# Latent attention of a macaron block: scores computed twice in two layouts instead of transposed probabilities, projections as three passes over high and low parts

## The chip, the cores and the metric

One NeuronCore of one Trainium2 chip runs the whole program. The metric is device time in microseconds (us), lower is better. Five engines work in parallel, each through its own list of instructions: TensorE (PE; its weight loads are PEld), VectorE (DVE), ScalarE (ACT), GpSimd (POOL) and SyncE (SP, transfers). They wait for one another through semaphores. TensorE writes only to PSUM, eight banks of 128 partitions by 512 fp32 values; GpSimd does not read PSUM.

## The reference

The input x is [8, 512, 128] (batch, token, channel). Three stages follow one another, each with a layer norm and a residual:

```python
x = x + 0.5 * ffn(layernorm(x))      # two layers, 8 heads, local attention over windows of 64 + GLU
x = x + mla(layernorm(x))            # latent attention, causal, 16 heads of 8 channels
x = x + 0.5 * ffn(layernorm(x))
```

Only the middle stage is touched by the change. It computes, per batch element:

```python
q      = x @ W_dq.T @ W_uq.T                       # [T, 16, 8]
c_kv   = x @ W_dkv.T
q_lat  = einsum('bqhd,hdl->bhql', q, k_eff)        # k_eff = W_dq.T W_uq.T W_uk
attn   = softmax(causal(q_lat @ c_kv.T / sqrt(8))) # [16, 512, 512], key <= query
y      = einsum('bhql,hld->bqhd', attn @ c_kv, v_eff)
```

The kernel folds the weight products once, so that each head has 8 query and 8 key channels and 8 value channels.

## The kernel before

`macaron` runs a setup, `ffn_phase`, `mla_phase` and `ffn_phase` again; X stays in SBUF throughout. In the trace `mla_phase` lies from 863 to 1341.5 us of the span; the two feed-forward phases fill nearly all the rest and aren't changed.

In `mla_phase` a **group** is 4 heads of one batch element: 8 batch elements by 4 groups are 32 groups. Every engine's program is written out in the same loop over `m`, with fixed lags between the stages: `m` runs over **units**, 11 to a group. A unit is a block i of 128 queries with n heads, whose scores fill one PSUM bank: one unit for i=0 (4 heads of 128 keys), two for i=1 (2 heads of 256), four each for i=2 and i=3 (one head of 384 or 512 keys).

- Per batch element (once in four groups): layer norm on DVE (L291 to L306), 4 transposes of U (L1066), a copy to XT (L1225), values for 16 heads (L1073, copied by ACT, L1162).
- Per group: the projection of queries (L1080) and of keys (L1086), each one matmul of 512 columns with fp32 operands. To keep fp32 accuracy in the cheaper fp32r matmuls of the scores, each head's 8 channels stand several times in 128 rows, as rounded value and as what rounding leaves: ACT rounds the projection to RND (L1170, L1177), DVE subtracts (QS L1232, KL L1250). QZL is QS with all rows but one head's set to zero, four copies: two by DVE (L1242), two by POOL (L1326).
- Scores: one fp32r matmul per head over all 128 rows (L1114), and one bf16 matmul of the causal mask onto the diagonal block (L1119). The group has 4 x (128+256+384+512) = 5120 columns of scores.
- Softmax: DVE takes the negated maximum of each row (NM, L1286); ACT writes exp(score + NM) to PL (L1205), one instruction per head.
- The probabilities are turned, 128x128 by 128x128, 40 transposes per group (L1128), and copied to PTL, 9 units of 11 by ACT (L1197), two by DVE (L1295).
- Output: probabilities times values, four blocks j of 128 keys, 4 heads each in 32 columns of the array (L1143), with a column of ones that gives the sums. Then a copy OTL (L1301), 4 transposes (L1155), a reciprocal and a product (L1306, L1309) on DVE, and the addition to X on POOL (L1333).

PSUM: banks 0 to 3 are a ring of scores, 4 and 5 take transposed probabilities, bank 6 (`B_O`) the output, bank 7 (`B_PREP`) all projections and small transposes, one after another. `claim` makes PE wait, before it writes a bank, for the reader of what it held:

```python
def claim(k, name, count):
    if readers[k]:
        pe.wait_ge(*readers[k])
    readers[k] = (S[name], count)
```

## Time and profile before

| | us |
|---|---|
| median of 3 runs | 2167.96 (2165.43 to 2172.27) |
| profiled execution, its own time | 2170.55 |
| span of the profiled execution | 2168.7 |
| PE busy | 1785.8 (82%) |
| DVE busy | 1488.3 (69%) |
| ACT busy | 1112.0 (51%) |
| POOL busy | 905.7 (42%) |
| `mla_phase`, first scores to last addition | 882.4 to 1341.5 |

Busy time of PE counts a matmul from its start to its modelled end, pipelined ones overlapping; how long one occupies the array is read from the distance between the starts of two that follow one another.

### The profile page before, as it was taken

What the parts mean: (1) busy time and instruction counts of PE and PEld (TensorE: products, weight loads), DVE (VectorE), ACT (ScalarE), POOL (GpSimd) and SP (SyncE); (2) the same over time, 40 slices, a digit from 0 to 9 for tenths busy, and PEclk for the clock granted to TensorE, in tenths of its full rate; (3) what the DMA queues carried; (4) which work ended last, traced back from release to release, by engine and by line L of the source; (5) the groups of instructions that cost most, each with busy time, mean ns of one, the idle gap of its engine ahead of it and who ended that gap; (6) DMA issues with size and microseconds to landing.
All of it is one profiled execution on the core that took longest, in us unless ns stands there. A gap on an engine that the chain in (4) does not pass through costs nothing. (4 is left out here: it accounts for less than half of the span.)

```text
span 2168.7 us, 50695 instructions
## 1 busy us (share of the span) xinstructions
PE 1785.8 (82%) x20074; PEld 1079.9 (50%) x20074; DVE 1488.3 (69%) x2281; ACT 1112.0 (51%) x2070; POOL 905.7 (42%) x624
## 2 busy tenths in 40 slices
PE   1578888888888886899999997578888888888885
PEld 1344444555555543566666664344454455555543
DVE  2567777677666753688888886567777677766752
ACT  1134444454544542688888886234444454544542
POOL 2445544555445540332233321445544555445530
PEclk9889999999999998899999998689999999999998
DMA  4234434544455441000000000334344544355441
GB/s 140 37 58 71 69 62 76 77 80 69 71 79 81 73 68 36 1 1 2 1 2 1 2 1 1 37 63 72 63 71 70 81 75 74 66 85 84 84 72 40
DMA packets 66076, 119.03 MB, mean 55 GB/s; under 512 B 13183, under 2 KB 23603, under 8 KB 63667
## 3 DMA queue, kind: packets, MB, share of 16 engines
q1 hardware_dynamic: 65843, 115.79, 31.8%
q8 instruction: 162, 2.65, 0.5%
q14 instruction: 71, 0.58, 0.1%
HBM read 49.55 MB, written 3.28 MB: 24 GB/s over the span
## 5 line engine op out<-in xcount | busy, mean ns | idle before, releaser
L786 DVE SCALAR_TENSOR_TENSOR TP<-bank,cols,tab 128x1024 f32<-128x1024 f32 x256 | 318.4, 1274 | 51.5 <-PE bank L450 42.5
L946 POOL TENSOR_TENSOR QK<-QK,RB 128x1024 f32<-128x1024 f32 x128 | 302.4, 2363 | 118.6 <-DMA RB<-RN 118.6
L940 POOL TENSOR_TENSOR QK<-TP 128x512 f32<-128x512 f32 x128 | 164.9, 1289 | 327.4 <-DVE TP L786 291.3
L1205 ACT ACTIVATE PL<-bank,NM 128x384 f32<-128x384 f32 (+3 forms) x512 | 255.7, 539 | 15.8 <-DVE NM L1286 13.0
L1286 DVE TENSOR_REDUCE NM<-bank 128x1 f32<-128x384 f32 (+3 forms) x352 | 217.9, 635 | 35.6 <-PE bank L1119 31.7
L809 DVE TRANSPOSE_TENSOR_REDUCE MX<-bank 128x16 f32<-128x512 f32 x256 | 160.2, 681 | 118.3 <-PE bank L487 118.3
L642 ACT ACTIVATE SQ<-bank 128x512 f32<-128x512 f32 x128 | 76.5, 598 | 275.7 <-PE bank L450 275.5
L1128 PE MATMUL bank<-cst,PL 128*128 128x128 f32 x1280 | 199.7, 275 | 3.6 <-DVE PTL L1295 1.4
L827 DVE TENSOR_TENSOR OT<-bank,OT 128x512 f32<-128x512 f32 x128 | 85.3, 687 | 160.9 <-DMA OT<-sums_d 146.9
L1114 PE MATMUL bank<-KL,QZL 128*128 128x384 f32 (+3 forms) x512 | 189.8, 422 | 2.3 <-DVE QZL L1242 2.3
L648 ACT ACTIVATE SQ<-bank 128x512 f32<-128x512 f32 x128 | 76.5, 598 | 201.2 <-DVE TP L786 201.2
L450 PE MATMUL bank<-HTH,wqkv_h 128*128 128x512 f32 x256 | 124.3, 486 | 54.8 <-DVE TP L786 43.6
L1197 ACT ACTIVATE PTL<-bank 128x512 f32<-128x512 f32 (+1 forms) x288 | 161.5, 561 | 13.2 <-PE bank L1128 9.7
L932 POOL TENSOR_TENSOR HTL<-Z,HTH 128x512 fp32r<-128x512 f32 x32 | 37.9, 1184 | 304.4 <-ACT HTH L636 304.4
L941 POOL TENSOR_TENSOR QK<-TP 128x512 f32<-128x512 f32 x128 | 164.4, 1284 | 0.0
L1326 POOL TENSOR_SCALAR QZL<-QS,cst 128x512 fp32r<-128x512 f32 x64 | 109.2, 1715 | 116.1 <-DVE QS L1232 116.0
L520 PEld LDWEIGHTS bank<-PT,V 128*64 128x64 f32 x4096 | 128.5, 138 | 53.2 <-issue 29.4
L487 PEld LDWEIGHTS bank<-QK 32*64 32x64 f32 x8192 | 133.9, 143 | 30.0 <-issue 30.0
L520 PE MATMUL bank<-PT,V 128*64 128x64 f32 x4096 | 140.1, 224 | 10.4 <-DVE OT L827 10.2
L487 PE MATMUL bank<-QK 32*64 32x128 f32 x8192 | 146.7, 291 | 0.0
L670 ACT ACTIVATE PT<-bank 128x512 f32<-128x512 f32 x256 | 132.1, 606 | 27.7 <-PE bank L501 27.7
L1128 PEld LDWEIGHTS bank<-cst,PL 128*128 128x128 f32 x1280 | 139.1, 141 | 8.9 <-issue 5.1
(169 smaller groups left out, 3655.8 us busy)
## 6 DMA issues: line engine op xcount, KB each, us to landing
RB<-RN SPq DMA_DIRECT2D x512, 64.0 KB, 4.0
OT<-sums_d SPq DMA_DIRECT2D x128, 256.0 KB, 4.0
V<-V SPq DMA_DIRECT2D x32, 512.0 KB, 6.0
V<-V SPq DMA_DIRECT2D x32, 384.0 KB, 7.1
RB<-vars_d SPq DMA_DIRECT2D x32, 256.0 KB, 3.2
X<-in_L_attn_x SPq DMA_DIRECT2D x8, 256.0 KB, 4.6
out<-X SPq DMA_DIRECT2D x8, 256.0 KB, 4.7
wqkv_raw<-in_L_ffn_wqkv SPq DMA_DIRECT2D x1, 1536.0 KB
```

The costliest lines, as they stand in the source:

```text
L487: last = nc.tensor.matmul(BK[i][e * W:(e + 1) * W, k0:k0 + n], QK[r, 2 * g + 1, z, k0:k0 + W], QK[r, 2 * g, z, k0:k0 + n], start=False, st ...
L520: last = nc.tensor.matmul(BK[k][e * W:(e + 1) * W, w * W:(w + 1) * W], (V1, V0)[w % 2][:, w // 2, h * DH:(h + 1) * DH], PT[:, j // 2, h % ...
L786: nc.vector.scalar_tensor_tensor(out=TP[:, o:o + 2, :], in0=BK[4 + z][:, :].unsqueeze(1).to_broadcast([P, 2, T]), scalar=q, in1=tab[:, e, ...
L809: last = nc.vector.tensor_reduce(MX[:, i, :], BK[i][:, :].rearrange("p (a b) -> p a b", b=32), AX_X, ALU.max, apply_transpose=True)
L940: nc.gpsimd.tensor_tensor(QK[:, m, 0, :], TP[:, 2, :], TP[:, 1, :], ALU.subtract)
L941: nc.gpsimd.tensor_tensor(QK[:, m, 1, :], TP[:, 0, :], TP[:, 3, :], ALU.add).then_inc(S["ad_ok"], 1)
L946: nc.gpsimd.tensor_tensor(QK[:, m, :, :], QK[:, m, :, :], RB[:, m, :].unsqueeze(1).to_broadcast([P, 2, T]), ALU.mult).then_inc(S["nr_ok"], 1)
L1114: nc.tensor.matmul(bank[:, h * N:(h + 1) * N], QZL[:, G % 2, h0 + h, i * P:(i + 1) * P].bitcast(F32R), KL[:, G % 2, 0:N].bitcast(F32R), st ...
L1128: last = pe.transpose(BK[B_PT[k % 2]][:, j * P:(j + 1) * P], PL[:, k % PRING, j * P:(j + 1) * P], ident)
L1197: nc.scalar.activation(dst, src, ACT.Copy).then_inc(S["pta_ok"], 1)
L1205: last = nc.scalar.activation(PL[:, m % PRING, h * N:(h + 1) * N], BK[m % SRING][:, h * N:(h + 1) * N], ACT.Exp, bias=NM[:, m % SRING, h:h ...
L1286: nc.vector.tensor_reduce(NM[:, m % SRING, 0:n], BK[m % SRING][:, 0:n * N].rearrange("p (h k) -> p h k", h=n), AX_X, ALU.max, negate=True) ...
```

## The change

In `mla_phase`:

- **Units** are now 2 heads each over a pair of neighbouring banks (`PAIR`), 6 to a group. Fill f=0 holds query block 3 (512 keys a head), f=1 blocks 2 and 0 (384+128), f=2 block 1 (256). For the turned scores f=0 holds key block 0 (512 queries), f=1 key blocks 3 and 1 (128+384), f=2 key block 2 (256).
- **First pass** (`scores`): two bf16 masks, then the scores. Each head now has 32 rows of its own in QS and KS, so the matmul reads 32 rows of the array instead of 128; QZL is gone. DVE only takes the maxima (`maxima`, 8 instructions a group where 11 were), into NM, one column in 32.
- **Turn of the maxima**: 4 transposes (`turn_max`) and one addition to QS (`add_max`), giving QC: row 24 of each head's 32 now holds minus the maximum; KS has a 1 there (`raw_k`'s bias `one_row`).
- **Second pass** (`scores_t`), `T_LAG` = 8 units behind the first: keys by queries, KS as weights and QC moving, then two masks, last. ACT takes the exponential straight into PTL, two heads in one instruction (`softmax_exp`). PL, the 40 transposes and their copies are gone.
- **Ring**: both passes take turns in three pairs of banks (`RING` = 3). Bank 6 also takes the turned output.
- **Projections**: x and the folded weights are split into high and low fp32r parts (`high_x` on ACT, `low_x` on DVE, once a batch element; `fold_h`, `fold_l` once); queries and keys are each three fp32r matmuls of 512 columns. ACT copies the sum to RAW; POOL makes the rows (`stack_q`, `stack_k`: two instructions each), two groups ahead of their use.
- The copy to OTL is ACT's. The setup sets two small blocks of the folded weights to zero and loads a second mask.

The core of the diff (indentation cut by 16 columns; the old loop body is in the listing above):

```diff
-UNITS = [(i, h0, n) for i, n in ((i, max(1, NT // (i + 1))) for i in range(NT))
-         for h0 in range(0, LG, n)]
-UN = len(UNITS)
-ON_DVE = [0, 0, 0, 0, 0, 0, 0, 0, 1, 0, 1]
+FILLS = [((3, 0),), ((2, 0), (0, 3 * P)), ((1, 0),)]
+DIAG = [(3 * P, T), (2 * P, T), (P, 2 * P)]
+FILLS_T = [((0, 0),), ((3, 0), (1, P)), ((2, 0),)]
+DIAG_T = [(0, P), (0, 2 * P), (0, P)]
+WIDTH_T = [T, T, 2 * P]
+AT_T = {j: n * T + o for n, fill in enumerate(FILLS_T) for j, o in fill}
+READY = {j: 2 * n + 2 for n, fill in enumerate(FILLS_T) for j, o in fill}
+UN = 2 * len(FILLS)
...
-PT_LAG, PV_LAG, YT_LAG = 3, 5, 11
-EV_LAG, OT_LAG, Y_LAG = 3, 8, 11
-SRING, PRING = 4, 4
-B_PT, B_O, B_PREP = (4, 5), 6, 7
-XT_AT, Q_AT, K_AT = 1, 3, 5
-ROUND_Q, ROUND_K = 2, 4
-STEPS = ALLU + YT_LAG + 1
...
+RING = 3
+B_O, B_PREP = 6, 7
+AHEAD, QRING, KRING = 2, 3, 4
+C_AT, Q_AT, K_AT = 1, 2, 4
+XT_AT, XL_AT, V_AT, VL_AT = (AHEAD, 0), (AHEAD, 1), (AHEAD, 5), (AHEAD + 1, 0)
+T_LAG = UN + 2
+PV_LAG = {0: T_LAG + 4, 1: T_LAG + 5, 3: T_LAG + 5, 2: T_LAG + 7}
+YT_LAG, Y_LAG = T_LAG + 8, T_LAG + 9
+STEPS = ALLU + Y_LAG + 1
...
+        def project(G, s):
+            b, g = divmod(G, GROUPS)
+            terms = ((fold_h, XTH), (fold_h, XTL), (fold_l, XTH))
+            for n, (w, h) in enumerate(terms):
+                last = nc.tensor.matmul(BK[B_PREP][:, :], w[:, s, g, :].bitcast(F32R),
+                                        h[:, b % 2, :].bitcast(F32R), start=(n == 0), stop=(n == 2))
+            return last
...
-            nc.tensor.matmul(BK[B_PREP][:, :], Wq_s[:, g, :, :], XT[:, b % 2, :],
-                             start=True, stop=True).then_inc(S["q_in"], 1)
...
+            project(G, 0).then_inc(S["q_in"], 1)
...
+            lo, hi = DIAG[f]
+            for e in range(2):
+                nc.tensor.matmul(pair[:, e, lo:hi], identb[:, :],
+                                 causalb[:, :].unsqueeze(1).to_broadcast([P, (hi - lo) // P, P]),
+                                 start=True, stop=False, skip_group_check=True)
+            for i, o in FILLS[f]:
+                N = (i + 1) * P
+                for e in range(2):
+                    rows = slice(32 * (h0 + e), 32 * (h0 + e) + 32)
+                    last = nc.tensor.matmul(pair[:, e, o:o + N],
+                                            QS[rows, G % QRING, i * P:(i + 1) * P].bitcast(F32R),
+                                            KS[rows, G % KRING, 0:N].bitcast(F32R),
+                                            start=False, stop=True, skip_group_check=True)
+            last.then_inc(S["s_in"], 1)
...
+        def turn_max(G):
+            pe.wait_ge(S["nm_ok"], UN * (G + 1))
+            claim(B_PREP, "qc_ok", G + 1)
+            for i in range(NT):
+                last = pe.transpose(BK[B_PREP][:, i * P:(i + 1) * P], NM[:, G % 2, i, :], ident)
+            last.then_inc(S["c_in"], 1)
...
+        def scores_t(m):
+            G, r = divmod(m, UN)
+            f, h0 = r // 2, r % 2 * 2
+            if r == 0:
+                pe.wait_ge(S["qc_ok"], G + 1)
+            pair = PAIR[place[0] % RING]
+            claim(place[0] % RING, "ex_ok", m + 1)
+            place[0] += 1
+            lo, hi = DIAG_T[f]
+            for j, o in FILLS_T[f]:
+                N = T - j * P
+                for e in range(2):
+                    rows = slice(32 * (h0 + e), 32 * (h0 + e) + 32)
+                    nc.tensor.matmul(pair[:, e, o:o + N],
+                                     KS[rows, G % KRING, j * P:(j + 1) * P].bitcast(F32R),
+                                     QC[rows, G % 2, j * P:T].bitcast(F32R),
+                                     start=(o == 0), stop=False, skip_group_check=True)
+            for e in range(2):
+                last = nc.tensor.matmul(pair[:, e, lo:hi], identb[:, :],
+                                        causaltb[:, :].unsqueeze(1).to_broadcast([P, (hi - lo) // P, P]),
+                                        start=False, stop=True, skip_group_check=True)
+            last.then_inc(S["t_in"], 1)
...
+                scores(m)
+            if 0 <= m - T_LAG < ALLU:
+                scores_t(m - T_LAG)
+            for j in PV_LAG:
+                g = group_at(m, PV_LAG[j])
+                if g is not None:
+                    attend(g, j)
...
+            nc.scalar.activation(RAW[:, 1, :], BK[B_PREP][:, :], ACT.Identity,
+                                 bias=one_row).then_inc(S["rk_ok"], 1)
...
+        def softmax_exp(m):
+            G, r = divmod(m, UN)
+            f, h0 = r // 2, r % 2 * 2
+            act.wait_ge(S["t_in"], m + 1)
+            if r == 0 and G >= 2:
+                act.wait_ge(S["o_in"], G - 1)
+            nc.scalar.activation(PTL[:, G % 2, h0:h0 + 2, f * T:f * T + WIDTH_T[f]],
+                                 PAIR[at_t(m) % RING][:, :, 0:WIDTH_T[f]], ACT.Exp).then_inc(S["ex_ok"], 1)
...
+        def maxima(m):
+            G, r = divmod(m, UN)
+            f, h0 = r // 2, r % 2 * 2
+            dve.wait_ge(S["s_in"], m + 1)
+            if r == 0 and G < 2:
+                dve.wait_ge(S["nm_zero"], 1)
+            if r == 0 and G >= 2:
+                dve.wait_ge(S["c_in"], G - 1)
+            for i, o in FILLS[f]:
+                last = nc.vector.tensor_reduce(NM[:, G % 2, i, 24 + 32 * h0:57 + 32 * h0:32],
+                                               PAIR[at(m) % RING][:, :, o:o + (i + 1) * P],
+                                               AX_X, ALU.max, negate=True)
+            last.then_inc(S["nm_ok"], 1)
...
+        def add_max(G):
+            dve.wait_ge(S["c_in"], G + 1)
...
+            nc.vector.tensor_tensor(QC[:, G % 2, :].bitcast(F32R), BK[B_PREP][:, :], QS[:, G % QRING, :],
+                                    ALU.add).then_inc(S["qc_ok"], 1)
...
-                nc.vector.tensor_copy(dst, src).then_inc(S["ptd_ok"], 1)
...
+        def stack_q(G):
+            pool.wait_ge(S["rq_ok"], G + 1)
+            link(nc.gpsimd.tensor_scalar(HI[:, 0, :].bitcast(F32R), RAW[:, 0, :], low_q, None, ALU.mult))
+            if G >= QRING:
+                pool.wait_ge(S["qc_ok"], G - QRING + 1)
+            nc.gpsimd.tensor_tensor(QS[:, G % QRING, :].bitcast(F32R), RAW[:, 0, :], HI[:, 0, :],
+                                    ALU.subtract).then_inc(S["qs_ok"], 1)
+        def stack_k(G):
+            pool.wait_ge(S["rk_ok"], G + 1)
+            link(nc.gpsimd.tensor_scalar(HI[:, 1, :].bitcast(F32R), RAW[:, 1, :], low_k, None, ALU.mult))
+            if G >= KRING:
+                pool.wait_ge(S["t_in"], UN * (G - KRING + 1))
+            nc.gpsimd.tensor_tensor(KS[:, G % KRING, :].bitcast(F32R), RAW[:, 1, :], HI[:, 1, :],
+                                    ALU.subtract).then_inc(S["ks_ok"], 1)
...
```

TensorE in the middle of the phase, **before**: from the projection of queries to the first blocks of output. QZL and KL are the operands of scores, PL the probabilities, PTL their transposes.

```order
L1080 MATMUL bank<-XT,fold 128x512
L1114 MATMUL bank<-KL,QZL 128x384
L1119 MATMUL bank<-causalb,identb 128x128
L1128 MATMUL bank<-cst,PL 128x128 x4
L1114 MATMUL bank<-KL,QZL 128x384
L1119 MATMUL bank<-causalb,identb 128x128
L1128 MATMUL bank<-cst,PL 128x128 x4
L1143 MATMUL bank<-PTL,VL 32x512 x4
L1086 MATMUL bank<-XT,fold 128x512
```

The same engine and place **in the changed program**, two steps of the loop (r = 2, with the projection of queries, and r = 3), up to the block of output behind them:

```order
L1093 MATMUL banks<-XTH,fold_h 128x512
L1093 MATMUL banks<-XTL,fold_h 128x512
L1093 MATMUL banks<-XTH,fold_l 128x512
L1121 MATMUL banks<-causalb,identb 128x256 x2
L1128 MATMUL banks<-KS,QS 128x384 x2
L1128 MATMUL banks<-KS,QS 128x128 x2
L1154 MATMUL banks<-QC,KS 128x512 x2
L1159 MATMUL banks<-causaltb,identb 128x128 x2
L1121 MATMUL banks<-causalb,identb 128x256 x2
L1128 MATMUL banks<-KS,QS 128x384 x2
L1128 MATMUL banks<-KS,QS 128x128 x2
L1154 MATMUL banks<-QC,KS 128x512 x2
```

The transposes of PL between the units are gone; each step has a unit of the first pass and one of the second, whose score matmuls stand next to each other, with masks on either side.

VectorE in the changed program, one group with no layer norm in it (L1325 is `add_max`, L1315 `maxima`, L1331 and L1334 the result):

```order
L1325 TENSOR_TENSOR QC<-banks,QS 128x512
L1315 TENSOR_REDUCE NM<-banks 128x2 x6
L1331 RECIPROCAL RL<-banks 128x16
L1334 TENSOR_TENSOR Y<-banks,RL 128x128
L1315 TENSOR_REDUCE NM<-banks 128x2 x2
```

Before, VectorE's list for a group held 11 such reductions, two copies to PTL, QS, KL, two QZL and OTL as well.

## Rows read from the trace of the kernel before

**Rows 1.** The page, part 1: busy time, share of the span, instructions.

```profile
PE 1785.8 (82%) x20074; PEld 1079.9 (50%) x20074; DVE 1488.3 (69%) x2281; ACT 1112.0 (51%) x2070; POOL 905.7 (42%) x624
```

**Rows 2.** Stretches: length, busy PE, PEld, DVE, ACT, POOL, clock, DMA, GB/s.

```profile
872.00:900.00 28.00, 22.87 (x110) 14.84 (x111) 17.46 (x39) 16.43 (x39) 7.52 (x5) 0.73 0.00 1
1100.00:1200.00 100.00, 98.90 (x772) 62.87 (x771) 84.23 (x169) 87.40 (x191) 29.51 (x23) 1.00 0.01 2
```

**Rows 3.** Line L1080, weight loads: min/median/max ns, first and last start.

```profile
L1080 PEld LDWEIGHTS bank<-XT,fold x64: 190/192/353, 874.5 to 1310.0; 128*128 128x128 f32 x64
```

**Rows 4.** Line L1333, the addition to X: min/median/max ns, first and last start.

```profile
L1333 POOL TENSOR_TENSOR X<-X,Y x32: 451/457/463, 909.9 to 1341.0; 128x128 f32<-128x128 f32 x32
```

**Rows 5.** Timeline of PE, start of the phase: start us, us, instruction.

```profile
869.78 1.11 PE L1066 MATMUL bank<-cst,U 128*128 128x128 f32 x4 [7.49 <-DVE U L306]
...
882.42 1.08 PE L1114 MATMUL bank<-KL,QZL 128*128 128x128 f32 x4 [2.31 <-DVE QZL L1242]
```

**Rows 6.** Timeline of PE, within one group in the middle of the phase.

```profile
1100.08 1.07 PE L1143 MATMUL bank<-PTL,VL 128*32 128x512 f32 x8
...
1101.08 1.12 PE L1086 MATMUL bank<-XT,fold 128*128 128x512 f32 x2
...
1102.22 0.23 PE L1119 MATMUL bank<-causalb,identb 128*128 128x128 bf16 x1
...
1103.95 0.50 PE L1128 MATMUL bank<-cst,PL 128*128 128x128 f32 x3
...
1104.38 0.64 PE L1143 MATMUL bank<-PTL,VL 128*32 128x256 f32 x8
...
1104.95 0.50 PE L1114 MATMUL bank<-KL,QZL 128*128 128x512 f32 x1
...
1107.45 0.47 PE L1114 MATMUL bank<-KL,QZL 128*128 128x512 f32 x1
1107.77 0.23 PE L1119 MATMUL bank<-causalb,identb 128*128 128x128 bf16 x1
1107.83 0.60 PE L1128 MATMUL bank<-cst,PL 128*128 128x128 f32 x4
1108.28 0.60 PE L1155 MATMUL bank<-cst,OTL 128*128 128x128 f32 x4
1108.63 0.64 PE L1114 MATMUL bank<-KL,QZL 128*128 128x128 f32 x4
1109.11 0.39 PE L1119 MATMUL bank<-causalb,identb 128*128 128x512 bf16 x1
1109.34 0.60 PE L1128 MATMUL bank<-cst,PL 128*128 128x128 f32 x4
```

**Rows 7.** Timeline of PE, first feed-forward phase: scores in small tiles of the array.

```profile
400.94 2.03 PE L487 MATMUL bank<-QK 32*64 32x128 f32 x128
402.90 1.07 PE L509 MATMUL bank<-PT,ones 128*32 128x512 f32 x8
```

**Rows 8.** The same phase: fp32r matmuls of 512 columns, four starts apart.

```profile
428.24 0.39 PE L450 MATMUL bank<-HTL,wqkv_h 128*128 128x512 f32 x1
...
429.18 0.40 PE L450 MATMUL bank<-HTH,wqkv_l 128*128 128x512 f32 x1
```

**Rows 9.** DVE by line and form, 900 to 1300 us: count, busy us, mean ns.

```profile
L1286 DVE TENSOR_REDUCE NM<-bank 128x1 f32<-128x512 f32 x112 | 73.0, 684 | 22.2 <-PE bank L1119 22.2
L1286 DVE TENSOR_REDUCE NM<-bank 128x1 f32<-128x384 f32 x113 | 62.3, 551 | 1.9
```

**Rows 10.** Timeline of DVE: three reductions in a row.

```profile
1135.70 1.88 DVE L1286 TENSOR_REDUCE NM<-bank 128x1 f32<-128x512 f32 x3
```

**Rows 11.** ACT by line and form, 900 to 1300 us.

```profile
L1205 ACT ACTIVATE PL<-bank,NM 128x512 f32<-128x512 f32 x112 | 77.8, 695 | 2.3 <-DVE NM L1286 1.7
```

**Rows 12.** POOL by line and form: L1326 from 868 to 1325 us.

```profile
L1326 POOL TENSOR_SCALAR QZL<-QS,cst 128x512 fp32r<-128x512 f32 x64 | 109.2, 1715 | 116.1 <-DVE QS L1232 116.0
```

**Rows 13.** POOL by line and form: L932, first feed-forward phase.

```profile
L932 POOL TENSOR_TENSOR HTL<-Z,HTH 128x512 fp32r<-128x512 f32 x16 | 18.9, 1184 | 150.9 <-ACT HTH L636 150.9
```

More of the change, by code:

```diff
@@ L49, in shape_constants @@
     causal = np.where(np.arange(P)[None, :] <= np.arange(P)[:, None], 0.0, BIG).astype(np.float32)
-    headsel = row % (LG * DG) // DG == np.arange(LG)[None, :]
-    low = [-1.0 * (row // (LG * DG) >= 2), -1.0 * (row // (LG * DG) % 2)]
+    part = row % 32 // DG
+    split = [part == 2, part == 1, row % 32 == 24]
     hsum = row // 32 == np.arange(32)[None, :] // 8
@@ L1008, in mla_phase, with group_at, at, at_t @@
+                def group_at(m, lag):
+                    G, r = divmod(m - lag, UN)
+                    return G if r == 0 and 0 <= G < ALLG else None
+                def at(m):
+                    return m + max(0, m - T_LAG)
+                def at_t(m):
+                    return min(m + T_LAG + 1, ALLU) + m
                 U = sb("U", [P, 2, NT, P])
                 fold = sb("fold", [P, 2 * GROUPS * P + P])
[L1010 removed]
@@ L1089, in _, with turn_out @@
+                        def turn_out(G):
+                            claim(B_O, "y_ok", G + 1)
+                            for t in range(NT):
+                                last = pe.transpose(BK[B_O][:, t * P:(t + 1) * P], OTL[:, t * P:(t + 1) * P], ident)
+                            last.then_inc(S["y_in"], 1)
                         xt(0)
                         pe.wait_ge(S["fold_in"], 16)
+                        for G in range(AHEAD):
+                            queries(G)
+                            keys(G)
@@ new lines, in _ @@
+                            if batch_at(m, VL_AT):
+                                values(batch_at(m, VL_AT))
+                            g = group_at(m, YT_LAG)
+                            if g is not None:
+                                turn_out(g)
+                            if r == Q_AT + 1 and G + AHEAD < ALLG:
+                                raw_q(G + AHEAD)
+                            if r == K_AT + 1 and G + AHEAD < ALLG:
+                                raw_k(G + AHEAD)
+                            if 0 <= m - T_LAG < ALLU:
+                                softmax_exp(m - T_LAG)
```

402 lines of the change are left out of this document (171 added, 231 removed).

## Prediction

> **What bounds the kernel now.** The page first: no engine fills the span, PE comes nearest with 82% [rows 1]. Only `mla_phase` changes, so its stretch is read by itself: between 1100 and 1200 us PE is busy 98.90 of 100 us at full clock, DVE 84.23, ACT 87.40, POOL 29.51 [rows 2]. PE never rests, so a group costs what PE needs for it. The first query projection loads its weights at 874.5, the last group's at 1310.0, 31 groups on [rows 3]: 14.05 us a group. From the first scores at 882.42 [rows 5] to the end of the last addition, 1341.0 + 0.46 [rows 4], are 459.0 us: 32 x 14.05 = 449.6 and 9.4 of lead and tail.
>
> **Prices on PE** are distances between starts. An fp32r matmul of 512 columns: (429.18 - 428.24) / 4 = 0.235 [rows 8]. A transpose: eight from 1107.83 to 1108.63, 0.10 each. A mask of 512 columns: 1109.34 - 1109.11 = 0.23. A score matmul of 512 columns behind a transpose: 0.32, so 0.08 of weight loading shows. Four of 128 columns: 1109.11 - 1108.63 = 0.48, 0.12 each, double the 0.06 of streaming: weights bound them. The fp32 projection: 1102.22 - 1101.08 = 1.14, less 0.26 for the score matmul of 384 columns between (0.32 less a quarter of 0.235), is 0.88. Output block of 256 columns: 1104.95 - 1104.38 = 0.57, of 512: 1101.08 - 1100.08 = 1.00; so 0.43 for each 256 columns and 0.14 fixed. In front of it three transposes from 1103.95 end by 1104.25, the block starts at 1104.38: 0.13 [rows 6]. The fixed 0.13 to 0.14 on either side is what I call a change of tile shape.
>
> Test on the old group: 44 transposes 4.4; scores and masks 4 x 0.38 + 4 x 0.32 + 2 x 0.44 + 0.71 = 4.4; output 1.00 + 0.78 + 0.57 + 0.35 and four entries of 0.13, 3.2; two projections 1.76; a quarter of the batch element's transposes and values, some 0.35. Sum 14.1 against 14.05: the prices hold.
>
> **The new group on PE.**
> - Transposes: 40 go, 4 come (the maxima), 4 stay: 8 x 0.10 = 0.80.
> - Projections: 6 x 0.235 = 1.41 instead of 1.76.
> - Masks: two passes of 2048 columns: 8 x 0.235 = 1.88.
> - Scores: 10240 columns, one after another 20 x 0.235 = 4.70. But two heads of a unit use different 32 rows of the array and different banks. No row of before has tiles of 32 x 128, so this is bounded. One end: no overlap, 4.70. The other: both heads at once, 2.35. The nearest row speaks for overlap: L487 has 64 fp32 matmuls in 32 x 64 tiles, 7680 columns, which at 0.88 for 512 would take 13.2 us in a row; they took 402.90 - 400.94 = 1.96, 6.7 times less with eight tiles [rows 7]. I take 2.35, and 0.25 for the 128-column ones.
> - Shape changes: since the masks of the second pass stand last, both passes' scores are adjacent, so a step has two changes, not four: 12 x 0.13 = 1.56.
> - Output: 2.70 as before, three blocks to enter instead of four: 2.9 in all. Batch share 0.35.
>
> Sum: 0.80 + 1.41 + 1.88 + 2.35 + 0.25 + 1.56 + 2.9 + 0.35 = 11.5 us.
>
> **The other engines must fit under that.** DVE: a reduction of 512 columns is 0.684, of 384 0.551, so 1.04 ns a column [rows 9], and in a row they follow every 0.60 (1.88 for three, the last one full) [rows 10]. One of 1024 then costs 1.13, f=1 (768 and 256 columns) 1.20, f=2 0.60; twice each 5.9. `add_max` 0.7, result 0.6, norm work, XT and the low part of x about 1.2 a group: 8.4. Two copies to PTL, QS, KL, QZL and OTL are gone. ACT: four exponentials of 1024, at most twice 0.695 [rows 11], two of 512, three copies: under 9.1. POOL: twice 1.72 + 1.18 [rows 12, 13] and 0.46 [rows 4]: 6.3; it works two groups ahead, so this is hidden, and if it came late the first scores of a group would wait. None bounds the group.
>
> **Waits.** `scores_t` of step m writes the pair that `scores` of m-1 had, so it waits for that maximum. It is tight where two f=1 units follow (r=2 to 3): the maximum comes 0.15 + 1.20 + 0.1 = 1.45 after the scores; PE has `scores_t` (0.235 + 0.12 + 0.13) and the next masks and scores (0.23 + 0.13 + 0.30) = 1.15 to do first, so it stands 0.3. Where norm work (0.3 to 0.45 a step, in every second group) lies between the reductions, 0.4 more there and some at r=5 to 0. Once a batch element DVE's XT, ACT's high part and DVE's low part stand in line before `add_max`: 0.5. Mean over groups: 0.6. `scores` of m waits for the exponential of m-2, at most 1.4, with over a step between: nothing. So 12.1 us a group.
>
> **Ends.** The lead changes little: x is split (ACT 0.6, DVE 0.7) and POOL makes rows in two times 2.9 in place of DVE's 0.75, but values come later: first scores near 881 instead of 882.4. The first 8 steps have no second pass and run at DVE's 1.2 a step instead of 2.0, 6.6 less; the last 8 units of the second pass with output and addition add 13.7. 7.1 in all instead of 9.4. Setup and feed-forward phases stay.
>
> **Sum.** 32 x (14.05 - 12.1) = 62.4, ends 2.3, start 1.4: 66 us off the profiled execution's 2170.55, 2104.5. The median is 2.6 lower, so **2102 us**. Within 0.3% (6.5 us) a measurement of this kernel can't tell a change.
>
> **A rule against it.** The shape change measured 0.13 [rows 6]. The Trainium skill, TensorEngine Tiling (Array Packing), Key Properties, says that changing the tiling mode drains TensorE; a full drain is the second rival below. At 0.13 a side the rows show less than that, though for 128 x 32 tiles only.
>
> **Rivals.**
> - *Waits small*: if weight loads hide behind the neighbouring head and waits cost nothing, 11.3 a group: 88 + 3.7 less, 2076. The 6.7-fold overlap [rows 7] speaks for it, the f=1 steps against.
> - *Full drain*: every change costs a transpose's time from start to end (0.60 for four, less three starts of 0.10: 0.30 [rows 6]) instead of 0.13: 12 x 0.17 = 2.0 more, PE then waits for nothing else, 13.5 a group: 2168 - 18 - 3.7, 2146. Output blocks of before speak against it.
> - *Maxima late*: the reductions over two banks or the exponentials come later than priced, 12.8 a group: 40 + 3.7 less, 2124. DVE's list has no slack at r=2 and 3.
> - *No overlap of heads*: 4.70 + 0.5 for scores, 14.1 to 14.2 with waits hidden: 2168 within 6. The change then doesn't do what 32-row tiles are there for. Rows 7 speak against it.
> - *Lockstep in the ring, slower*: three pairs for two passes. If each step is PE's first-pass fill, wait, maximum, second-pass fill one after another (0.65 + 0.15 + 1.0 + 0.1 + 0.55 = 2.45 a step, everything else hidden), a group is 14.7: 21 more, less 3.7 at the ends, 2185. It decides from 14.05 / 6 = 2.34 us a step. Against it: `scores` of m doesn't need the maximum of m-1, so PE can fill ahead.
>
> **Chances.** Forecast (11.7 to 12.4 a group, 2090 to 2114) 0.45, waits small 0.2, maxima late 0.18, full drain 0.06, no overlap 0.04, lockstep 0.07. All but the last two are faster: 0.89; same 0.04; slower 0.07. The range takes in the forecast, most of the small-wait and of the late-maxima case: 2080 to 2135.
>
> **What would show it.** `mla_phase` from first scores to last addition 394 us; distance of two `turn_max` 12.1; PE busy near all of it at clock 1.00 (in the lead it is 0.73 [rows 2] and should be so again); score matmuls of a pair starting far closer than 0.235 apart; PE waiting for NM at the second f=1 step and hardly elsewhere; DVE near 70%, ACT near 65%, POOL 50%. I am wrong if the pair starts 0.235 apart, if a shape change costs 0.3, or if PE waits for NM or PTL in every step.

## The result and the profile after

The changed kernel takes 2141.97 us (median of 3 runs, 2140.03 to 2146.62) against 2167.96: ratio 0.988, 95% interval 0.9852 to 0.9908, 26 us faster. The forecast was 2102, range 2080 to 2135. The sign is right, the gain is 40% of what was forecast, and the time lies outside the range. The profiled execution took 2146.62 with a span of 2144.8.

The page of the changed kernel, part 1, answers to [rows 1]:

```profile
PE 1746.9 (81%) x19914; PEld 1024.5 (48%) x19914; DVE 1369.1 (64%) x2002; ACT 938.8 (44%) x1503; POOL 979.3 (46%) x692
```

Stretches of the changed kernel (length, busy PE, PEld, DVE, ACT, POOL, clock, DMA, GB/s); the first two are those of [rows 2]:

```profile
872.00:900.00 28.00, 17.09 (x53) 10.01 (x54) 9.78 (x26) 5.46 (x8) 19.95 (x15) 0.54 0.06 22
1100.00:1200.00 100.00, 93.44 (x789) 53.15 (x789) 63.33 (x116) 53.74 (x73) 50.14 (x41) 0.98 0.00 1
...
880.00:900.00 20.00, 15.34 (x45) 8.88 (x46) 5.43 (x11) 4.40 (x7) 17.32 (x14) 0.50 0.00 1
900.00:920.00 20.00, 19.88 (x88) 10.61 (x87) 12.92 (x24) 6.46 (x8) 10.59 (x8) 0.50 0.00 1
920.00:940.00 20.00, 18.41 (x126) 10.24 (x122) 9.05 (x15) 7.93 (x11) 6.08 (x5) 0.78 0.00 1
940.00:960.00 20.00, 19.53 (x174) 11.06 (x174) 13.32 (x27) 10.95 (x15) 8.91 (x7) 1.00 0.00 1
```

Two things show. In the middle PE has 6.6 us of idle time in 100, where before it had 1.1. And from 880 to 920 the granted clock is 0.50 (1.2 GHz), even in the 20 us from 900 in which PE is busy 19.88, and from 920 to 940 still 0.78. Before, with its first scores at 882.42, it was back at 1.00 by 888:

```profile
884.00:888.00 4.00, 4.00 (x17) 2.36 (x17) 3.49 (x11) 2.84 (x9) 0.62 (x1) 0.59 0.00 0
888.00:892.00 4.00, 3.53 (x23) 2.29 (x22) 4.00 (x9) 3.80 (x9) 3.79 (x3) 1.00 0.00 0
```

The turn of the maxima (L1138, `turn_max`) happens once a group, so the distance between two of them is the time of a group. Here are four of them in the middle of the phase, in the PE timeline of the changed kernel. PE stood longest ahead of the third, for XT, and ahead of L1085, the matmuls that make a batch element's values:

```profile
1055.02 0.66 PE L1138 MATMUL banks<-cst,NM 128*128 128x128 f32 x4
...
1067.13 0.66 PE L1138 MATMUL banks<-cst,NM 128*128 128x128 f32 x4
...
1080.80 0.63 PE L1138 MATMUL banks<-cst,NM 128*128 128x128 f32 x4 [0.68 <-DVE XT L1297]
...
1091.27 1.13 PE L1085 MATMUL banks<-fold,XT 128*128 128x128 f32 x8 [1.35 <-ACT RAW L1235]
...
1095.24 0.66 PE L1138 MATMUL banks<-cst,NM 128*128 128x128 f32 x4
```

The distances are 12.11, 13.67 and 14.44; the next one, which completes the four groups of a batch element, is 11.98. A **plain** group costs 11.98 or 12.12 by turns, 12.05 on average. The two groups in which the next batch element is prepared cost 13.67 and 14.43, together 4.0 more. The first two distances of the phase are 17.02 and 17.79.

Why PE waits 1.35 for ACT stands in ACT's timeline there. The key projection was finished about 1088.4. ACT copied it (L1235) only at 1090.45, behind the exponential of the projection's own step (L1244), and that exponential had waited for its scores:

```profile
1089.53 1.02 ACT L1244 ACTIVATE PTL<-banks 128x1024 f32<-128x1024 f32 x1 [1.00 <-PE banks L1159]
1090.45 0.68 ACT L1235 ACTIVATE RAW<-banks,cst 128x512 f32<-128x512 f32 x1
```

The prices within a plain group, PE timeline (answers to [rows 6]):

```profile
1097.70 0.50 PE L1093 MATMUL banks<-XTH,fold_h 128*128 128x512 f32 x1
1098.04 0.39 PE L1093 MATMUL banks<-XTL,fold_h 128*128 128x512 f32 x1
1098.27 0.40 PE L1093 MATMUL banks<-XTH,fold_l 128*128 128x512 f32 x1
1098.51 0.39 PE L1121 MATMUL banks<-causalb,identb 128*128 128x256 bf16 x2
1098.83 0.50 PE L1128 MATMUL banks<-KS,QS 32*128 32x384 f32 x4
1099.17 0.45 PE L1154 MATMUL banks<-QC,KS 32*128 32x512 f32 x2
1099.55 0.28 PE L1159 MATMUL banks<-causaltb,identb 128*128 128x128 bf16 x2
1099.67 0.38 PE L1121 MATMUL banks<-causalb,identb 128*128 128x256 bf16 x2
1099.98 0.51 PE L1128 MATMUL banks<-KS,QS 32*128 32x384 f32 x4
1100.72 0.49 PE L1154 MATMUL banks<-QC,KS 32*128 32x512 f32 x2 [0.23 <-DVE NM L1315]
```

Three passes of a projection take 0.81 (1097.70 to 1098.51). Both heads' first-pass scores, 1024 columns, take 0.34 (1098.83 to 1099.17); at 0.235 for 512 they would take 0.47 if one followed the other. Two masks with the change of shape behind them take 0.32, and PE waits for a maximum once, 0.23, in the second f=1 step.

### The profile page after: what moved, and what is told of

The parts are those of the page before. It is cut to its first block and busy times, and to the rows that moved or that the text cites. A ratio compares the mean times of both kernels' runs of the same rounds, so it can differ in the third digit from the quotient of the medians.

```text
span 2144.8 us, 48275 instructions
## 1 busy us (share of the span) xinstructions
PE 1746.9 (81%) x19914; PEld 1024.5 (48%) x19914; DVE 1369.1 (64%) x2002; ACT 938.8 (44%) x1503; POOL 979.3 (46%) x692
## 3 DMA queue, kind: packets, MB, share of 16 engines
q8 instruction: 160, 2.62, 0.5%
## 5 line engine op out<-in xcount | busy, mean ns | idle before, releaser
L793 DVE SCALAR_TENSOR_TENSOR TP<-banks,cols,tab 128x1024 f32<-128x1024 f32 x256 | 318.3, 1274 | 52.5 <-PE banks L457 46.5
L1315 DVE TENSOR_REDUCE NM<-banks 128x2 f32<-128x1024 f32 (+3 forms) x256 | 202.9, 820 | 129.4 <-PE banks L1128 129.4
L1244 ACT ACTIVATE PTL<-banks 128x1024 f32<-128x1024 f32 (+1 forms) x192 | 168.1, 884 | 192.9 <-PE banks L1159 190.5
L816 DVE TRANSPOSE_TENSOR_REDUCE MX<-banks 128x16 f32<-128x512 f32 x256 | 160.2, 682 | 122.3 <-PE banks L494 122.3
L649 ACT ACTIVATE SQ<-banks 128x512 f32<-128x512 f32 x128 | 76.6, 599 | 279.1 <-PE banks L457 278.8
L655 ACT ACTIVATE SQ<-banks 128x512 f32<-128x512 f32 x128 | 76.7, 599 | 200.3 <-DVE TP L793 200.3
L527 PEld LDWEIGHTS banks<-PT,V 128*64 128x64 f32 x4096 | 128.6, 138 | 52.9 <-issue 29.5
L494 PEld LDWEIGHTS banks<-QK 32*64 32x64 f32 x8192 | 136.3, 145 | 30.3 <-issue 30.3
L494 PE MATMUL banks<-QK 32*64 32x128 f32 x8192 | 149.2, 294 | 0.0
L527 PE MATMUL banks<-PT,V 128*64 128x64 f32 x4096 | 140.2, 224 | 9.9 <-DVE OT L834 9.7
L677 ACT ACTIVATE PT<-banks 128x512 f32<-128x512 f32 x256 | 132.4, 609 | 27.7 <-PE banks L508 27.4
```

The source lines that it names most:

```text
L494: last = nc.tensor.matmul(BK[i][e * W:(e + 1) * W, k0:k0 + n], QK[r, 2 * g + 1, z, k0:k0 + W], QK[r, 2 * g, z, k0:k0 + n], start=False, st ...
L527: last = nc.tensor.matmul(BK[k][e * W:(e + 1) * W, w * W:(w + 1) * W], (V1, V0)[w % 2][:, w // 2, h * DH:(h + 1) * DH], PT[:, j // 2, h % ...
L677: nc.scalar.activation(PT[:, g, i, :], BK[i][:, :], ACT.Exp).then_inc(S["ex_ok"], 1)
L793: nc.vector.scalar_tensor_tensor(out=TP[:, o:o + 2, :], in0=BK[4 + z][:, :].unsqueeze(1).to_broadcast([P, 2, T]), scalar=q, in1=tab[:, e, ...
L816: last = nc.vector.tensor_reduce(MX[:, i, :], BK[i][:, :].rearrange("p (a b) -> p a b", b=32), AX_X, ALU.max, apply_transpose=True)
L1244: nc.scalar.activation(PTL[:, G % 2, h0:h0 + 2, f * T:f * T + WIDTH_T[f]], PAIR[at_t(m) % RING][:, :, 0:WIDTH_T[f]], ACT.Exp).then_inc(S[" ...
```

## The experiments

Twelve more kernels ran. Ratios are to runs of the kernel before that were taken together with each, so ratios compare better than medians. **Phase** is the distance from VectorE's first statistics of `mla_phase` to the start of the last turn of maxima: it leaves out the feed-forward phases, whose code no kernel here touches. Phase and distances come from one profiled execution of each kernel; the change and e8 are the same kernel, and their phases differ by 1.1. "First two distances" are those between the first three turns of maxima.

| run | median us | ratio [95%] | phase us | first two distances, us |
|---|---|---|---|---|
| the change | 2141.97 | 0.988 [0.9852, 0.9908] | 436.0 | 17.02, 17.79 |
| e8 change again | 2139.79 | 0.9855 [0.9813, 0.9897] | 434.9 | 17.02, 16.96 |
| e1 values later | 2128.55 | 0.9802 [0.9771, 0.9832] | 424.3 | 17.01, 14.07 |
| e2 e1 and XT first | 2122.08 | 0.977 [0.974, 0.9801] | 419.9 | 17.02, 13.97 |
| e6 copies early | 2122.91 | 0.9756 [0.9724, 0.9788] | 414.3 | 16.80, 13.57 |
| e3 the change, lead filled | 2135.12 | 0.9831 [0.9799, 0.9863] | 435.8 | 17.02, 17.75 |
| e9 e6, first 8 steps filled | 2117.19 | 0.9743 [0.9714, 0.9772] | 407.9 | 10.52, 12.89 |
| e7 e6, lead and steps filled | 2109.80 | 0.9701 [0.9673, 0.9728] | 406.8 | 10.66, 12.89 |
| e11 e7, values behind | 2115.30 | 0.9731 [0.9705, 0.9756] | 410.9 | 16.71, 13.63 |
| e12 e11, root earlier | 2113.91 | 0.9728 [0.9681, 0.9774] | 404.2 | 10.62, 12.87 |
| e5 fp32 projection | 2149.24 | 0.9883 [0.9847, 0.992] | 445.5 | 17.82, 15.71 |
| e4 masks first | 2181.61 | 1.005 [1.0026, 1.0074] | 477.8 | 18.66, 18.11 |
| e10 same rows | 2304.04 | 1.0611 [1.0552, 1.0671] | 588.6 | 21.27, 22.75 |

### The change once more (e8)

> The change itself once more, on the chip of the three others: 2142 within 7. If the start of the phase at 874.0 in its first profile was chance of the clock in the first feed-forward phase, it lies between 860 and 870 here, and the span from there to the end stays 1270.8 within 3; if it belongs to the change, it is 874 again.

The phase began at 861.75, not at 874.01, so the 10.7 us by which the first profile's phase began later than before (863.35) aren't the change's. The span from there to the end was 1265.2, not within 3 of the first profile's 1270.8 (before, 2168.7 - 863.35 = 1305.4): the second feed-forward phase varies too. That the clock in the feed-forward phases does this isn't shown.

### Where the once-a-batch time goes (e1, e2, e6)

```diff
-XT_AT, XL_AT, V_AT, VL_AT = (AHEAD, 0), (AHEAD, 1), (AHEAD, 5), (AHEAD + 1, 0)
+XT_AT, XL_AT, V_AT, VL_AT = (AHEAD, 0), (AHEAD, 1), (AHEAD + 1, 0), (AHEAD + 1, 0)
```

> Theory A: once per batch element the values (L1085) stand right behind the keys' projection in bank 7 and wait 1.35 to 1.5 us for ACT's RAW copy, which stands behind an exponential. The values move one step on (r = 5 to r = 0 of the next group); the copy is then done. The 14.4 us group falls by 1.5 to about 12.9, seven times: some 10 us less than the changed kernel, about 2132. Rival B: the stall only moves, since the maxima's turn at r = 1 then waits for the copy to VL: the group stays within 0.3 of 14.4, and the time at 2142.

The group of 14.43 became 13.40, where 12.9 was expected; all others of the middle stayed, and the second distance fell from 17.79 to 14.07. By the medians of e8 and of the change, e1 is 11 to 13 us faster; seven times 1.03 are the shorter group. In the phase, 10.6 us shorter than e8's, the rest is groups that had run at the low clock: the second distance, and e8's group of 15.95.

e2 is e1 with `xt` ahead of `maxima` in VectorE's step:

> As e1, and DVE copies XT before the maxima of that step, not behind them. Theory A: the 0.7 us that the maxima's turn waits for XT goes too, the 13.7 us group falls to about 13.0, 5 us less than e1, about 2127. Rival B: the maxima come 0.7 later instead and the second pass of r = 1 waits for them: same as e1.

The group of 13.67 became 12.92, as expected: 0.75 of it was the place of XT in VectorE's list.

e6 starts from the change and mends ACT's order, the cause of the longest wait, together with the place of XT; the values stay in step r=5 of their group:

```diff
-if r == Q_AT + 1 and G + AHEAD < ALLG:
+if r == Q_AT and G + AHEAD < ALLG:
     raw_q(G + AHEAD)
-if r == K_AT + 1 and G + AHEAD < ALLG:
+if r == K_AT and G + AHEAD < ALLG:
     raw_k(G + AHEAD)
...
-XT_AT, XL_AT, V_AT, VL_AT = (AHEAD, 0), (AHEAD, 1), (AHEAD, 5), (AHEAD + 1, 0)
+XT_AT, XL_AT, V_AT, VL_AT = (AHEAD, 0), (AHEAD, 1), (AHEAD, 5), (AHEAD, 5)
...
+if batch_at(m, XT_AT):
+    xt(batch_at(m, XT_AT))
 if m < ALLU:
     maxima(m)
-if batch_at(m, XT_AT):
-    xt(batch_at(m, XT_AT))
```

> ACT's copies of the projections (RAW) stand in the same step as the projections, ahead of that step's exponential, the copy of the values in the step of the values, and DVE's XT ahead of the maxima of its step; values stay at r=5 on TensorE. Theory A, the once-a-batch stall is a bank held by a copy that stands behind an exponential on ACT: the wait of 1.35 at the values and of 0.31 at the transposes of U go, the groups of 14.43 and 13.67 become 13.1 and 12.6, seven times 2.4 = 17 us, and without the stall no low clock in the middle: 2117 to 2124. Rival B, the copy waits for the projection itself, not for its place: values still wait over 1 us, gain under 5 us.

PE timeline of e6 with three turns of maxima, and between them the transposes of U (L1078) and the values (L1085), which have no wait left:

```profile
1055.43 0.66 PE L1138 MATMUL banks<-cst,NM 128*128 128x128 f32 x4
...
1065.61 0.66 PE L1078 MATMUL banks<-cst,U 128*128 128x128 f32 x4
...
1068.06 0.66 PE L1138 MATMUL banks<-cst,NM 128*128 128x128 f32 x4
...
1077.06 1.06 PE L1085 MATMUL banks<-fold,XT 128*128 128x128 f32 x8
...
1080.94 0.66 PE L1138 MATMUL banks<-cst,NM 128*128 128x128 f32 x4
```

The groups cost 12.63 and 12.88 instead of 13.67 and 14.44: 2.6 less a batch element, 18 us over seven. Theory A of that expectation holds and rival B falls, but 0.75 of the 2.6 is XT's place by e2, and the other 1.85 ACT's copies. What is left above a plain group is 1.4, which is the work itself (0.43 for four transposes, 0.97 for the values). In the middle PE is now busy 98 of 100 us, and the low clock there is gone:

```profile
1050.00:1150.00 100.00, 98.11 (x847) 55.45 (x843) 67.59 (x121) 58.65 (x78) 51.16 (x43) 1.00 0.00 1
```

### The low clock of the first groups (e3, e9, e7)

All three add bf16 matmuls of 512 columns over all 128 rows, which nothing reads: `fill(n)` issues n of them. The **lead** is what TensorE does before the first scores. e3 starts from the change and has 17 of them in the lead, into bank 5. e7 starts from e6 and has 26 in the lead and 16 in the first eight steps; e9 is e7 without those of the lead. The diff is e7's:

```diff
+def fill(n):
+    for _ in range(n):
+        nc.tensor.matmul(BK[B_O][:, :], identb[:, :], bandb[:, :], start=True, stop=True,
+                         skip_group_check=True)
 xt(0)
 pe.wait_ge(S["fold_in"], 16)
+fill(6)
 for G in range(AHEAD):
     queries(G)
+    fill(4)
     keys(G)
+    fill(4)
 values(0)
+fill(4)
...
+if m < T_LAG:
+    fill(2)
 if 0 <= m - T_LAG < ALLU:
     scores_t(m - T_LAG)
```

> Seventeen dummy matmuls of 512 bf16 columns fill PE's pauses before the first scores; they write a bank that nobody reads, and add nothing to the result. Theory A: the array stood mostly idle from 878 to 893 us and so entered the scores at 1.2 GHz, and stayed there to about 925; kept busy it is at 2.4 GHz when the scores begin and stays there. First scores to the third turn of the maxima (893.4 to 938.4, 45 us) then take about 32; 10 to 14 us less than the changed kernel, about 2130. Rival B: what keeps the clock down is not the pause but the new stream itself (masks and 32-row scores, no second pass yet): the clock falls or stays at 0.5 until the second pass sets in, the gain is under 4 us.

In e3 the lead ran at full clock from 874, and the first scores (885.07) came 18.1 us after the phase began instead of 19.4. But the clock fell at 891, in the steps that have a first pass only, and the first two distances were still 17.02 and 17.75. Rival B of e3 holds: the phase is 435.8, no shorter than the change's, and its median, 7 us below the change's, owes nothing to that. The waits of PE around the fall, in the timeline of e3 (the last comes behind it):

```profile
889.32 0.50 PE L1093 MATMUL banks<-XTH,fold_h 128*128 128x512 f32 x1 [0.77 <-ACT RAW L1237]
...
891.57 0.37 PE L1121 MATMUL banks<-causalb,identb 128*128 128x128 bf16 x2 [0.31 <-POOL KS L1396]
...
893.40 1.11 PE L1138 MATMUL banks<-cst,NM 128*128 128x128 f32 x4 [0.74 <-DVE NM L1323]
```

Later its clock fell again behind the stall at L1085, and two groups took 17.27 and 13.65. So an early full clock doesn't last by itself. e7 filled the lead and those steps, e9 the steps alone:

> The run before, and 26 extra bf16 matmuls of 512 columns over all 128 rows into bank 6 in the lead and two in each of the first eight steps, whose results nothing reads. Theory A, the clock falls and stays low because TensorE stands still in the lead and has only 32-row scores and masks in the first eight steps: clock 1.00 from about 876 on, the first two distances 12 to 13 instead of 17.0 and 14 to 17.8, first scores within 1 us of 18 after the phase starts; 6 to 10 us faster than the run before. Rival B, the clock is low after the phase change whatever TensorE does: first distances stay at 17, and the extra matmuls cost 0.5 us each at half clock, up to 8 us slower than the run before.

> The run with early copies and filling, without the extra matmuls of the lead: only the two in each of the first eight steps are left. Theory A1, the clock is lost in the lead's standing still and full-row matmuls in the steps are enough to bring it back: 1.00 within a few us after the first scores, second distance 12.9, first distance under 14, within 5 us of 2110. Theory A2, both stretches must be filled: the clock stays at 0.50 through the eight steps, where the extra matmuls then cost about 8 x 2 x 0.2 = 3 us more, first distance 17 or more: 2122 to 2127. It tells which part of the filling earned the 13 us.

Stretches of e7:

```profile
876.00:880.00 4.00, 4.00 (x15) 1.92 (x14) 0.00 (x0) 1.28 (x2) 3.66 (x4) 0.79 0.00 0
880.00:900.00 20.00, 18.87 (x114) 10.26 (x116) 14.53 (x28) 5.63 (x8) 18.70 (x14) 1.00 0.00 1
900.00:920.00 20.00, 19.77 (x176) 11.42 (x175) 13.35 (x19) 11.46 (x17) 8.94 (x7) 1.00 0.00 1
```

and of e9:

```profile
880.00:884.00 4.00, 3.13 (x13) 2.24 (x12) 0.00 (x0) 1.28 (x2) 3.92 (x3) 0.50 0.00 0
884.00:888.00 4.00, 3.67 (x13) 1.92 (x13) 2.83 (x4) 0.00 (x0) 3.92 (x3) 0.53 0.01 4
888.00:892.00 4.00, 4.00 (x27) 2.14 (x27) 3.13 (x8) 1.28 (x2) 2.99 (x3) 1.00 0.00 0
```

In e9, with its first scores at 883.30, the clock is back at 1.00 by 888, when only the first few of the sixteen useless matmuls have run; in e6 it came back 28.5 us after the first scores (from 891.48 to 920.0). The first two distances fall from e6's 30.4 us together to 23.4, and the phase is 6.5 shorter than in e6. With the lead filled as well it is 1.1 shorter still, no more than the phases of the change and of e8 differ. By the clock and the distances theory A1 of e9 holds, and of e7 theory A. Parts of both were missed: e9's median is 2117.19, not within 5 of 2110, and its ratio isn't separated from e6's; e7's first scores came 19.8 us after the phase began, not 18, and its median is 13 below e6's, not 6 to 10. The profiled spans of e7 and e9 differ by 1.1, like their phases (2109.6 and 2110.7); what made their medians differ by 7.4 isn't shown.

### The order of the masks (e4)

Second pass: masks first, scores behind them, so that no two passes' scores stand together and a step has four changes of shape.

```diff
+for e in range(2):
+    nc.tensor.matmul(pair[:, e, lo:hi], identb[:, :],
+                     causaltb[:, :].unsqueeze(1).to_broadcast([P, (hi - lo) // P, P]),
+                     start=True, stop=False, skip_group_check=True)
 for j, o in FILLS_T[f]:
...
-                         start=(o == 0), stop=False, skip_group_check=True)
-for e in range(2):
-    last = nc.tensor.matmul(pair[:, e, lo:hi], identb[:, :],
-                            causaltb[:, :].unsqueeze(1).to_broadcast([P, (hi - lo) // P, P]),
-                            start=False, stop=True, skip_group_check=True)
+                         start=False, stop=True, skip_group_check=True)
```

> The masks of the second pass stand first, as in the first pass, so a step has four changes of tile shape instead of two. Theory A (a change costs 0.10 to 0.14 us as read from the rows): 12 more changes a group, 1.2 to 1.7 us, 38 to 54 us in all, about 2188. Rival B (the array starts a matmul of another shape without a pause, and the 0.1 is only the weight load that shows): under 10 us more. Rival C (a change drains the array, 0.3 each): 110 us more, above 2250.

A plain group takes 13.03 instead of 12.05: 0.98 for twelve changes, and the wait of 0.23 at the f=1 step is gone under them, so (0.98 + 0.23) / 12 = 0.10 each. Theory A's range of 0.10 to 0.14 just holds, and its rivals fall. e4 gives the price of a change; whether the array stands empty or a weight load shows in those 0.10 it doesn't tell. Masks placed last are worth 31 us by that (32 x 0.98), and 37 to 40 by ratio and median, with the clock, which fell oftener (groups of 18.27, 18.16 and 18.66 behind stalls at L1085). Without this placing the change would be no gain: ratio 1.005.

### The projection (e5)

```diff
-terms = ((fold_h, XTH), (fold_h, XTL), (fold_l, XTH))
-for n, (w, h) in enumerate(terms):
-    last = nc.tensor.matmul(BK[B_PREP][:, :], w[:, s, g, :].bitcast(F32R),
-                            h[:, b % 2, :].bitcast(F32R), start=(n == 0), stop=(n == 2))
-return last
+return nc.tensor.matmul(BK[B_PREP][:, :], Wqk_s[:, s, g, :], XT[:, b % 2, :],
+                        start=True, stop=True)
```

> The projection part of the change undone: queries and keys are again one matmul of 512 columns with fp32 operands on XT, the high and low parts of x and of the folded weights are not made. If three fp32r passes and one fp32 matmul cost what the starts showed (0.81 with their weights against 0.88), a plain group is 0.1 to 0.2 longer (11.98 to 12.15), 4 to 5 us in all, and the once-a-batch chain shorter by ACT's high and DVE's low part where turn_max waits for DVE: 13.67 and 14.43 stay within 0.3. The first scores come 1 to 3 us earlier, since the lead has no splits. Sum within 6 us of the change (2137 to 2148). Rival, three passes are the dearer form because their weight loads show: groups 0.3 shorter, 2130.

PE timeline of e5:

```profile
1052.70 1.12 PE L1091 MATMUL banks<-XT,fold 128*128 128x512 f32 x2
1053.66 0.38 PE L1116 MATMUL banks<-causalb,identb 128*128 128x256 bf16 x2
```

A projection takes 0.96 instead of 0.81. Plain groups are 12.28 and 12.41, 0.3 longer, more than the 0.1 to 0.2 expected, and the phase is 10.5 longer than in e8. The first scores came 20.1 us after the phase began, not 1 to 3 earlier than the change's 19.4 but 0.8 later, and the median is just past the expected 2148. The rival falls: three passes are the cheaper form. Splitting x costs the chain little, since the two groups with a batch element's preparation are longer by the same 0.3 without it (13.97 and 14.75).

### Both heads in the same rows (e10)

```diff
-rows = slice(32 * (h0 + e), 32 * (h0 + e) + 32)
+rows = slice(32 * h0, 32 * h0 + 32)
```

> The change, but both heads of a unit are computed in the 32 rows of the first (head h0 twice, h0+1 not at all), so that their matmuls can't stand side by side in the array; banks, sizes, masks and waits as before. Theory A, the two heads run at once and half of the scores' columns are free: 10240 columns then cost 20 x 0.235 = 4.70 instead of 2.35 and a group is 2.35 to 2.6 longer, 11.98 becomes 14.3 to 14.6, 32 x 2.4 = 77: 2210 to 2225. Rival B, the starts in the trace only look close since an issue queue lets them start early: under 0.5 a group, 2140 to 2158.

PE timeline of e10, the pair of 512 columns:

```profile
1027.24 0.73 PE L1128 MATMUL banks<-KS,QS 32*128 32x512 f32 x2
1027.82 0.39 PE L1154 MATMUL banks<-QC,KS 32*128 32x256 f32 x2
```

The pair takes 0.58 where the change has 0.34: one more matmul. At full clock the plain groups are 14.06 and 14.07, 2.0 longer, where 2.35 to 2.6 were expected; the wait of 0.24 at the f=1 step is gone under them. So theory A holds, and heads side by side in the array are worth 64 us (32 x 2.0). But the median of 2304.04 is far above the expected 2210 to 2225: by the ratios e10 is 158 us slower than the change, and by the phase 152.6. Its other groups take up to 22.76, at a clock whose mean is 0.82 from 960 to 1300. Stretches of e10, in which PE has no wait:

```profile
1080.00:1082.00 2.00, 2.00 (x13) 1.13 (x12) 1.62 (x3) 1.38 (x2) 0.00 (x0) 1.00 0.00 0
1082.00:1084.00 2.00, 2.00 (x13) 0.99 (x13) 0.85 (x2) 1.75 (x3) 1.69 (x2) 0.54 0.00 0
1084.00:1086.00 2.00, 2.00 (x9) 1.28 (x8) 0.16 (x1) 0.00 (x0) 1.15 (x1) 0.50 0.00 0
```

### Towards a better version (e11, e12)

e11 is e7 with the first values behind the first scores:

```diff
-values(0)
-fill(4)
 for m in range(STEPS):
...
 if m < ALLU:
     scores(m)
+if m == 0:
+    values(0)
```

> The run with early copies and filling (2109.8), with the values of the first batch element behind the first scores instead of ahead of them, and without the four extra matmuls there. If TensorE's own order gates the first scores, they come 1.5 to 3 us earlier (19.6 after the phase starts becomes 17 to 18) and all behind them too: 2107 to 2108. Rival, the first rows of keys from POOL gate them: no change.

The first scores came 16.4 us after the phase began instead of 19.8, 3.4 earlier where 1.5 to 3 were expected. Yet the phase was 4.1 longer, and the median 2115.30 instead of 2107 to 2108. PE's and VectorE's timelines of e11 say why:

```profile
895.26 0.50 PE L1154 MATMUL banks<-QC,KS 32*128 32x512 f32 x2 [2.62 <-DVE NM L1326]
...
893.28 0.72 DVE L313 TENSOR_SCALAR U<-X,mv,rstd 128x128 f32<-128x128 f32 x1 [2.40 <-POOL rstd L309]
```

POOL worked without a pause and took the square root of the next batch element only after the rows of group 2's queries and keys. VectorE's norm work waited for it, with the maxima behind it, PE stood 2.62 us, and the clock was 0.50 from 896.3 to 906.5. e12 takes the root earlier:

```diff
-if n % GROUPS == 1 and n // GROUPS + 1 < NB:
-    norm_rstd(pool, S, n // GROUPS + 1)
 if n + AHEAD < ALLG:
     stack_q(n + AHEAD)
+if n % GROUPS == 0 and n // GROUPS + 1 < NB:
+    norm_rstd(pool, S, n // GROUPS + 1)
+if n + AHEAD < ALLG:
     stack_k(n + AHEAD)
```

> The run with the values behind the first scores, and on POOL the square root of the next batch element (L309) between the rows of queries and of keys of group 0 instead of behind both. Theory: in that run TensorE stood 2.62 us at the second pass, because DVE stood 2.40 us for POOL's root, which had two instructions of rows in front of it; and the clock fell to 0.50 from that stall on. Then the stall goes, the clock stays at 1.00 and the first two distances are 10.7 to 12.9 again: 3 us below the run with early copies and filling, 7 below the one with values behind: 2106 to 2109. Rival, POOL's rows themselves come too late: a stall of over 1 us stays at another place, the clock falls as before, 2113 to 2116.

The stall is gone, the clock stays at 1.00, and the phase is 404.2: 6.7 below e11 and 2.6 below e7, as expected. The median isn't: it is 2113.91, not 2106 to 2109, and its four times lie between 2108.41 and 2120.76. So by the medians neither e11 and e12 nor e7 and e12 are separated (their intervals overlap), and that e12 is the best of them rests on the phase alone. All three are faster than the change and the kernel before.

## Why the prediction was right or wrong

**`mla_phase` took 35.5 us more than forecast.** From the first scores (893.38) to the end of the last addition (1322.85) are 429.5 us, forecast 394, before 459.0. There are 31 distances of `turn_max`. The 27 from the third on take 351.0 where 27 x 12.1 = 326.7 were forecast, 24.3 more; the first two 34.8 instead of 24.2; the last two 20.6 instead of 24.2; the ends make up the other 4. Of the 24.3, 11.2 are point 1, 11.7 point 3, and the rest one group of 15.96 at the low clock.

1. *"Once a batch element ... stand in line before `add_max`: 0.5"* is the step that failed first. With 4 x 0.35 of work I had 1.9 a batch element; it is 4.0. Six batch elements fall in those 27 groups, 24.0 us, where 27 / 4 x 1.9 = 12.8 were forecast: 11.2 more. The work was right (1.4 in e6); the waits are 2.6 instead of 0.5. I followed VectorE's chain and never asked who holds bank 7: the key copy stands on ACT behind an exponential, and transposes, values and `turn_max` queue for the bank in turn. e6 moved the copies and XT and took all 2.6 away, of which VectorE's part, the one that I had priced, is 0.75 by e2. Seven times 2.6 is 18 of the 20.6 us of phase between e8 and e6; the medians differ by 17.
2. *"PE busy near all of it at clock 1.00 (in the lead it is 0.73 ...)"* failed too. Before, TensorE was in steady work soon after 882, and the clock was 1.00 from 888. After, the lead has waits at every projection and eight steps hold little but 32-row scores and masks, and the clock stayed at 0.50 to about 921. *"The first 8 steps ... run at DVE's 1.2 a step"* fell with it: the seven steps from the first scores to the first turn took 10.18 us, 1.45 each; in e3, most of them at full clock, 8.33, 1.19 each. With the clock held (e7) the first two distances are 23.6 instead of 34.8; 4.4 of these 11 us came with e6. e9, which differs from e6 in nothing but what TensorE is given in those eight steps, shows the part of the clock: 7.0.
3. *The new group on PE, 11.5.* Without the batch share and its waits I had 11.62; it is 12.05, 11.7 us over 27 groups. Term by term: projections 1.61 for 1.41 (0.34 for the first pass, whose entry I didn't count), eight transposes 0.93 for 0.80, output 2.57 for 2.9, masks, scores and changes 6.7 for 6.04, waits 0.24 for 0.3 at the f=1 step and some 0.2 elsewhere. It is a mis-sizing of 4%, by errors of both signs; the largest term of it, 0.67 for masks, scores and changes, isn't taken apart further.
4. *Heads side by side, 2.35* held: 0.34 for two heads' 512 columns, and e10 shows what the other end would have cost. The 6.7-fold overlap of [rows 7] was the right row.
5. *Shape change 0.13, twelve a group* held on the safe side: 0.10 (e4). The Trainium skill, TensorEngine Tiling (Array Packing), Key Properties, has it that switching the tiling mode drains TensorE. e4 doesn't contradict it and gives the switch a price, 0.10 us between 32-row and 128-row tiles, a third of what the rival had.
6. *"PE waiting for NM at the second f=1 step and hardly elsewhere"* held: 0.23 against 0.3.
7. *DVE near 70%, ACT near 65%, POOL 50%*: 63, 54 and 50 of 100 us. With the batch share a group there lasts 13.05, so DVE works 8.3 us a group, as priced (8.4), and ACT 7.0, less than the bound of 9.1.
8. *The start 1.4 us earlier*: it came 0.3 us later by its own measure (893.38 - 874.01 = 19.4 after the phase began; 882.42 - 863.35 = 19.1 before). In the lead every later projection waits 0.69 or 0.87 us for ACT's copy of the one before, at half clock; at full clock (e3) it was 18.1.

The number came out near the rival "full drain" (2146) and in none of its ways: a change costs 0.10, not 0.30. "Maxima late" isn't it either: the only such wait is 0.23. No rival had the bank that is held by a late copy, and none had the clock. With both mended, e7's ratio of 0.9701 makes 2103 of the 2167.96, next to the forecast's 2102, but that is in part luck: from first scores to last addition e7 takes 399.8, still 6 above the forecast's 394, and 59.2 less than before, where the ratio says 65.

The range was too narrow because each of its ends varied a price or a wait inside a group that I had already listed. Nothing in it stood for a wait at a place I hadn't looked at, although the whole order of four engines was new.

## What to carry to other kernels

When a bank or buffer passes through many hands, write down for each holder what stands ahead of its release on the releasing engine; a copy behind an instruction that itself waits is a stall, and moving it one place earlier is free. When a change leaves TensorE with thin work or short waits in a stretch, look at the granted clock there before pricing it: the gain of faster code can be given back at 1.2 GHz, and a few full-width matmuls that nobody reads can pay for themselves. Bringing work forward (e11) helps only if every engine of the chain comes along.
